# Windowed attention on one core: the two rows of maxima of a step sent through two queues and awaited apart

## What is computed

```python
H, W = 16, 128                      # heads, window
B, L, D = x.shape                   # 4, 2048, 512
E, nw = D // H, L // W              # 32, 16 windows
q, k, v = split(x @ w_qkv)          # each B, H, nw, W, E
k_ctx = concatenate([pad(k)[:, :, i:i + nw] for i in range(3)], axis=3)
v_ctx = concatenate([pad(v)[:, :, i:i + nw] for i in range(3)], axis=3)
scores = einsum('bhnqe,bhnke->bhnqk', q * E ** -0.5, k_ctx)
attn = softmax(where(valid, scores, -1e9))
out = einsum('bhnqk,bhnke->bhnqe', attn, v_ctx)
```

## Time and profile before

| | us |
|---|---|
| median of 3 runs | 2949.45 |
| lowest, highest | 2947.25, 2953.7 |
| the profiled execution's own time | 2945.01 |
| its span in the trace | 2943.2 |
| PE busy over the span | 2872.6 (98%) |
| ACT busy | 1731.4 (59%) |
| DVE busy | 1997.2 (68%) |
| mean granted TensorE clock | 0.992 of full speed |

### The profile page before, as it was taken

One profiled execution on the slowest core, in us unless ns is written; L12 is line 12 of the kernel. 1 busy time (PEld: TensorE's weight loads), 2 busy tenths in 40 slices (PEclk: granted clock), 3 DMA queues, 4 the chain that ended last, 5 costly groups with the idle time before them and its releaser, 6 DMA issues.

```text
span 2943.2 us, 55585 instructions
## 1 busy us (share of the span) xinstructions
PE 2872.6 (98%) x20380; PEld 2397.3 (81%) x20380; DVE 1997.2 (68%) x3769; ACT 1731.4 (59%) x3385; POOL 854.8 (29%) x715
## 2 busy tenths in 40 slices
PE   8999999999999999989989999999999999999998
PEld 6888888788888888778868888888888888888886
DVE  5333333488888887888868766876768766786664
ACT  3222222367767676665636666866668666676666
POOL 1000000188888888874400000500005000040003
PEclk9999999999999999999989999999999999999999
DMA  6555555677888889959998866986669755795642
GB/s 215 185 172 171 186 188 193 215 189 193 195 197 194 196 196 228 217 178 393 397 386 338 292 207 209 357 308 210 240 209 404 273 203 202 286 399 198 233 136 86
DMA packets 361429, 697.10 MB, mean 237 GB/s; under 512 B 26576, under 2 KB 127056, under 8 KB 361184
## 3 DMA queue, kind: packets, MB, share of 16 engines
q1 hardware_dynamic: 336464, 629.89, 66.4%
q10 hardware_dynamic: 16416, 31.98, 3.1%
q0 software_dynamic: 8304, 31.98, 2.7%
HBM read 525.45 MB, written 167.78 MB: 236 GB/s over the span
## 4 chain that ended last, share of the span: by engine, by line
PE 82%; DMA 6%; DVE 4%; issue 2%; ACT 2%; SPq 2%; POOL 1%; ACTq 0%; DVEq 0%; POOLq 0%
PE a_acc L574 17%; PE e_hid L1394 7%; PE e_hid L1392 7%; PE e_hid L1393 7%; PE e_acc L1409 7%; PE e_acc L1411 7%; PE e_acc L1410 7%; PE a_ps_keys L642 5%; PE a_ps_score L625 5%; PE a_ps_out L671 5%; DMA a_q_st<-a_max_rows 3%; DMA a_gate_att<-o_scratch 3%; PE a_ps_out L679 1%; DVE e_part L1782 1%; PE a_turn L569 1%
## 5 line engine op out<-in xcount | busy, mean ns | idle before, releaser
L1782 DVE SCALAR_TENSOR_TENSOR e_part<-e_ring,e_g_cols,e_part 128x512 f32<-128x512 f32 x896 | 647.6, 777 | 4.6 <-DMA e_ring<-mix_rows 2.2
L491 DVE TENSOR_REDUCE a_neg_max<-a_ps_score 128x1 f32<-128x384 f32 (+1 forms) x1024 | 491.8, 526 | 64.0 <-PE a_ps_score L625 53.0
L329 POOL TENSOR_TENSOR a_total<-a_probs 128x512 f32<-128x512 f32 x256 | 324.1, 1283 | 593.3 <-ACT a_probs L421 593.2
L421 ACT ACTIVATE a_probs<-a_ps_keys 128x384 f32<-128x384 f32 (+1 forms) x1024 | 427.1, 478 | 53.7 <-PE a_ps_keys L642 27.3
L1806 DVE TENSOR_TENSOR e_u_lo<-e_u,e_u_hi 128x512 fp32r<-128x512 f32 x256 | 180.0, 703 | 373.8 <-ACT e_u_hi L1540 373.6
L1536 ACT ACTIVATE e_u<-e_hid,e_mb 128x512 f32<-128x512 f32 x256 | 176.9, 691 | 433.8 <-PE e_hid L1394 421.2
L1265 POOL TENSOR_SCALAR e_var<-e_moments 128x4 f32<-128x4 f32 x15 | 6.7, 447 | 1275.5 <-DVE e_moments L1818 1274.8
L642 PE MATMUL a_ps_keys<-a_q_st,a_k_st 97*128 97x384 f32 (+1 forms) x1024 | 314.4, 349 | 16.5 <-DMA a_q_st<-a_max_rows 15.3
L625 PE MATMUL a_ps_score<-a_k_st,a_q_st 96*128 96x384 f32 (+1 forms) x1024 | 327.6, 358 | 2.7 <-DVE a_neg_max L491 2.5
L339 POOL TENSOR_TENSOR a_total<-a_total,a_probs 128x512 f32<-128x512 f32 x224 | 286.1, 1279 | 63.6 <-ACT a_probs L421 61.2
L471 DVE TENSOR_TENSOR a_qk<-a_acc,a_qk 128x512 fp32r<-128x512 f32 x128 | 88.0, 690 | 308.0 <-ACT a_qk L370 308.0
(11 more groups left out here) (158 smaller groups left out, 6506.0 us busy)
## 6 DMA issues: line engine op xcount, KB each, us to landing
e_ring<-mix_rows SPq DMA_DIRECT2D x558, 512.0 KB, 5.4
qk_scratch<-a_qk SPq DMA_DIRECT2D x128, 512.0 KB, 3.2
a_k_st<-qk_scratch SPq DMA_DIRECT2D x180, 256.0 KB, 4.4
a_q_st<-qk_scratch SPq DMA_DIRECT2D x180, 256.0 KB, 4.5
v_scratch<-a_v SPq DMA_DIRECT2D x64, 256.0 KB, 3.0
a_v_sb<-v_scratch SPq DMA_DIRECT2D x64, 256.0 KB, 4.9
o_scratch<-a_out SPq DMA_DIRECT2D x128, 128.0 KB, 3.0
x_scratch<-a_gate_x POOLq DMA_DIRECT2D x16, 1024.0 KB, 10.2
```

What stands on the lines that cost most here:

```text
L329: add = pool.tensor_tensor(total[:, g % 2, i], p[0], p[1], ALU.add)
L421: act.activation(probs[:, m % PROBS, h, 0:(hi - lo) * WIN], ps_keys[x % TRIO][:, 0:(hi - lo) * WIN], ACT.Exp, scale=SCALE).then_inc(exp_do ...
L491: dve.tensor_reduce(neg_max[:, g % 2, i, h:h + 1], ps_score[y % TRIO][:, 0:(hi - lo) * WIN], AX_X, ALU.max, negate=True).then_inc(reduced, 1)
L1782: dve.scalar_tensor_tensor(out=part[:, n % 2, half, :], in0=ring[:, slot, :], scalar=g_cols[:, b, e:e + 1], in1=so_far, op0=ALU.mult, op1= ...
```

## The change

- The two rows of a step have a semaphore each, for each parity of the step (`rows_landed[i][g % 2]`).
- In the steps, the first row is issued by ACT, after exponential 4 of T (each issue waits for `rows_done`); the second by SP, at the place where both stood. The rows of steps 0 and 1, in the front, both stay with SP.
- TensorE awaits the first row of step g+1 ahead of keys 4 of step g, and the second row of step g+1 ahead of keys 0 of step g+1, in every step.
- `copy_rows` waits for the two semaphores of step g-2, one after the other.

```diff
-        rows_landed = [sem(f"rows_landed{i}") for i in range(2)]
+        rows_landed = [[sem(f"rows_landed{i}{p}") for p in range(2)] for i in range(2)]
...
+        def send_row(eng, g, i):
+            w = 2 * (g % HALF) + i
+            eng.wait_ge(rows_done, g + 1)
+            eng.dma_start(q_st[STACK:STACK + 1, :, w * WIN:(w + 1) * WIN].bitcast(F32),
+                          max_rows[QH * i:QH * (i + 1), g % 2, :].bitcast(F32)).then_inc(rows_landed[i][g % 2], 16)
...
-            def row(g):
-
-                sp.wait_ge(rows_done, g + 1)
-                w = 2 * (g % HALF)
-                for i in range(2):
-                    sp.dma_start(q_st[STACK:STACK + 1, :, (w + i) * WIN:(w + i + 1) * WIN].bitcast(F32),
-                                 max_rows[QH * i:QH * (i + 1), g % 2, :].bitcast(F32)).then_inc(rows_landed[g % 2], 16)
...
                 if g == 5:
-                    row(0)
-            row(1)
+                    for i in range(2):
+                        send_row(sp, 0, i)
+            for i in range(2):
+                send_row(sp, 1, i)
...
                 if there(T + AHEAD - 1):
-                    row(T + AHEAD - 1)
+                    send_row(sp, T + AHEAD - 1, 1)
...
                     if there(T):
                         weights(T, x)
+                    if x == 4 and there(T + AHEAD - 1):
+                        send_row(act, T + AHEAD - 1, 0)
...
                 if g >= 2:
-                    dve.wait_ge(rows_landed[g % 2], 32 * (g // 2))
+                    for i in range(2):
+                        dve.wait_ge(rows_landed[i][g % 2], 16 * (g // 2))
...
                 if x == 0 and g % HALF == 0:
-                    pe.wait_ge(rows_landed[g % 2], 32 * (g // 2 + 1))
+                    pe.wait_ge(rows_landed[0][g % 2], 16 * (g // 2 + 1))
+                if x == 0:
+                    pe.wait_ge(rows_landed[1][g % 2], 16 * (g // 2 + 1))
                 if x == QH and g % HALF != HALF - 1:
-                    pe.wait_ge(rows_landed[(g + 1) % 2], 32 * ((g + 1) // 2 + 1))
+                    pe.wait_ge(rows_landed[0][(g + 1) % 2], 16 * ((g + 1) // 2 + 1))
```

## The result

The changed kernel took 2942.21 us in the median of 20 runs, the kernel before 2949.85 in as many (2949.75 without one run of 10 ms, which was disturbed). The ratio is 0.9976, with a 95% interval of 0.9967 to 0.9986. Forecast were 2931 us, 18.3 less than before; measured are 7 to 8 less. The direction and the range hold, the size doesn't.

A forecast was written before the change was run, and what follows sets the result against it. TensorE was taken as the bound, its row waits costing 24.6 us. -24.6 + 6.3 = -18.3 us took the profiled execution from 2945.0 to 2926.7; that execution lies 4.4 us under the median, so 2931 was forecast, range 2922 to 2960.

The forecast's parts named there:

- What bounds the kernel, and what a wait is worth: Attention: TensorE is the bound, DVE isn't; 26 steps with row waits cost 24.6 us, all the change can win.
- The second row, with its wait 2 us later: Awaited at keys 0 of the next step, it gets about 2.0 us more; its waits were taken as gone.
- The first row, the term of -24.6 us: Sent from ACT's own queue, it lands in 3 us or less, and all 26 waits at keys 4 go: -24.6 us.
- Rival B: The first row's landing doesn't depend on the queue, only the earlier issue helps: 9 us gained, 2940 us; chance 0.18.
- the rule weighed there: Skill's queue rule: SP and ACT rings share 16 transfer engines, served packet by packet, so the row passes SP's loads.
- ScalarE's issue, +6.3 us: The row's issue between exponentials 4 and 5 is covered but for 0.05 us, reaching TensorE in 126 steps: +6.3 us.
- D: The length for which issuing a row blocks ACT, taken as 0.60 us.
- VectorE's second wait, "nothing": The added row wait in `copy_rows` comes where DVE idles 0.72 us for TensorE, so it costs nothing.
- TensorE's additional wait, nothing: The added wait at keys 0 of each step, already met and covered by products in flight, costs nothing; uncovered, 6 us.

The follow-up runs named there:

- change_again: The changed kernel once more, unaltered, for a second profile; ratio 0.9969 to the kernel before.
- after_loads_late: The changed kernel with SP's row issued ahead of the step's loads instead of behind them; ratio 0.9991 to the kernel before.
- act_unsplit: The changed kernel without the split: ScalarE sends the first row, both rows are awaited at keys 4; ratio 1.0002 to the kernel before.
- all_three: The changed kernel with VectorE's row waits ahead of the step's first three reductions and the load of v behind SP's row; ratio 0.9944 to the kernel before.
- all_three_sp: all_three with the first row issued by SP again, ahead of the second; ratio 0.9933 to the kernel before.
- dve_early: The changed kernel with VectorE's two row waits moved ahead of the step's first three reductions; ratio 0.9938 to the kernel before.
- before_dve_early: The kernel before with VectorE's wait for both rows moved ahead of the step's first three reductions; ratio 0.9971 to the kernel before.
- along_early: all_three with the 512 KB loads of the late steps issued ahead of the step's store; 2923.96 us, ratio 0.9892 to the kernel before.

## Why the prediction was wrong in size

- *What bounds the kernel, and what a wait is worth:* held in part. TensorE's path sets the time, and a long wait can cost more than its length, because the granted clock falls behind it; but not always (it fell behind one of 1.7 us before, and stayed at 1.00 behind one of 2.3 us in change_again, in a step of 7.61 us). That VectorE "isn't the bound" was misread: the same table had 20.4 us of TensorE's waits for reductions. So the 24.6 us of the long steps were all that the waits for rows could give, and there was more to win that I hadn't looked for, in the clean steps.
- *The second row, with its wait 2 us later:* held, but for the one wait of 1.3 us at keys 0 in one of two profiles.
- **The first row, the term of -24.6 us:** this is the step that failed. "On a queue of its own, with nothing in front of it, I expect 3 us or less". It took 5.3 us in the wait shown and 3.4 in the mean of the 100 middle steps, from the end of its issue, and 15.4 to 17.9 us of the 22.7 us of waits stayed. (The 4.1 and 7.05 us that I had from SP's queue count from the issue's start; from its end they are 3.5 and 6.5.) Rival B had it: the landing doesn't depend on the queue. The transfer that matters is not the one in front in the queue but the loads in flight on the same transfer engines, as after_loads_late shows. B was even too mild: it kept "the earlier issue helps", 1.7 us of it; in the mean, what keys 4 awaits landed 0.2 us earlier. That B's 2940 lies near the measured 2942 is partly luck: it is made of a gain of 15.6 us and a price of 6.3, and neither was found.
- *On the rule weighed there:* the Trainium skill (DMA: Bandwidth & Descriptors) has both sides. Its section Issuing engines are not separate DMA queues, that a second issuing engine saves only the time of issue, is borne out: the row landed 5.02 us after the turning from ScalarE's queue and 4.90 from SP's, and act_unsplit gained nothing (1.0002). Its packet-by-packet round between rings would let a transfer of 2 KB pass the loads once a packet of theirs is through; in the wait shown nothing of the row moved for 1.7 us, and it did not pass the loads in the mean either. How long such a packet lasts no run here shows. The section on queues also says that an increment lands only after the earlier writes of that transfer engine, from whatever queue; that the last count came 0.98 us behind the row's data in the change and 0.55 in after_loads_late is in line with it, though no run here isolates it, and it is the smaller part of the delay.
- **ScalarE's issue, +6.3 us:** mis-sized. D was 0.58 as estimated, but the issue starts 0.03 us before exponential 4, beside exponential 3, so a little more of it is hidden; all_three against all_three_sp shows 0 to 0.01 us a step.
- **VectorE's second wait, "nothing":** wrong, and this is where the 3.8 us (0.03 x 126) were lost which I had put down to ScalarE. An engine that idles is no cover for a wait on the path. The copy starts 0.31, 0.38 or 0.41 us after the turning with none, one or two other waits ahead of it, though they were met long before.
- *TensorE's additional wait, nothing:* held (dve_early has it, 5.33; before_dve_early doesn't, 5.33).

What the measured 7 us are made of isn't settled. In the two profiles of the change, the step of 9.17 us at 583 takes 6.9 and 6.1, the 100 middle steps are 0 and 1.0 us shorter, and the 21 late ones 4.3 us longer and 1.5 shorter: together a loss of 2.0 and a gain of 5.5. The profile of before is itself of a quick execution (2945.0 against a median of 2949.85), and which late waits end in a lower clock differs from one execution to the next. That the change saves falls of the clock in the slower executions would fit, but it is not shown: there is no profile of one.

## What to carry to other kernels

In this kernel a small transfer that someone waits for landed when the bulk issued ahead of it landed; a queue of its own didn't lift it out. Order the issues instead, the urgent load, the small transfer, then the load that has time, and look at what becomes late in its place: with all loads behind the rows, q was. And in a loop in which one engine waits for another's result, keep other waits, even those long met, out of the place directly ahead of it; ask it of each semaphore that an edit adds, on every engine.

## What the runs showed of the hardware that I had not expected

- A wait on a semaphore that was met long ago cost VectorE 0.07 us where it was the first beside the wait that counts, and 0.03 us more where it was the second, even out of 0.7 us of idleness. On TensorE, with products in flight, an additional met wait cost nothing.
- A 2 KB transfer on an idle queue took 5.3 us from the end of its issue to its landing while another queue's loads of 256 KB were in flight. It was slower than a transfer of the same size issued later behind such loads in the kernel before (3.5 us); both landed at the same moment of the step. Over 100 steps it took 3.4 us from ScalarE's queue beside the loads and 1.5 us with the loads issued later.
- An issue of 0.58 us on ScalarE delayed the next of a row of exponentials by only 0.23 us (0.60 from 4 to 5 instead of 0.37): it ran beside the exponentials ahead.
- The late steps at full grant (along_early) take TensorE 4.8 us less busy time for the same 1738 products than those with a grant of 0.96 (114.94 against 119.76): where the clock falls behind a wait, the products behind it take longer as well.
